# Scores of two layers as eight small TensorE tiles: four batches over four PSUM banks a step

## What is computed

```python
def layer(x, ctx, mask, Wq, Wk, Wv, Wo, gamma, beta, gate):   # x, ctx: (64, 64, 256)
    a = layer_norm(ctx, gamma, beta)
    Q, K, V = (heads(t @ W.T) for t, W in ((x, Wq), (a, Wk), (a, Wv)))   # 16 heads of 16 features
    scores = einsum('bhtd,bhsd->bhts', Q, K) * 16 ** -0.5
    attn = softmax(where(mask, scores, -inf), axis=-1)
    out = einsum('bhts,bhsd->bhtd', attn, V)
    return x + tanh(gate) * (out.reshape(x.shape) @ Wo.T)
```

## Time and profile before

| | |
|---|---|
| median of 3 runs | 643.26 us (642.9 to 643.43) |
| profiled execution: first to last instruction | 641.2 us |
| its own time | not listed apart; the runs are about 2.1 us above its span |
| PE busy | 612.8 us |
| DVE busy | 481.5 us |
| ACT busy | 486.4 us |
| one turn of the loop | 74.8 us |

### The profile page before, as it was taken

The page is one execution under the profiler, slowest core; times in us unless marked ns, Lnnn a source line. Parts: engine busy times, 40 slices in busy tenths (PEclk is TensorE's granted clock), DMA queues, the critical chain, the costliest instruction groups (busy, mean ns, idle before and its releaser), DMA issues.

```text
span 641.2 us, 22171 instructions
## 1 busy us (share of the span) xinstructions
PE 612.8 (96%) x9027; PEld 556.5 (87%) x9027; DVE 481.5 (75%) x1069; ACT 486.4 (76%) x945; POOL 119.4 (19%) x136
## 2 busy tenths in 40 slices
PE   1799999999999999999999999999999999999996
PEld 1688899989898898988999898988989899899885
DVE  4866778785986869777787859868697777876475
ACT  0998778776876969767787768869697677877682
POOL 3602420007010060104300070100601043000000
PEclk9999999999999999999999999999999999999999
DMA  5420002000021000110020000200001100000001
GB/s 159 143 71 2 3 3 73 9 28 2 2 73 34 2 1 24 51 34 2 2 73 13 23 2 2 73 34 2 2 17 56 35 2 1 3 14 23 3 2 34
DMA packets 18485, 18.09 MB, mean 28 GB/s; under 512 B 1828, under 2 KB 18340, under 8 KB 18404
## 3 DMA queue, kind: packets, MB, share of 16 engines
q1 hardware_dynamic: 18024, 16.55, 8.1%
q0 software_dynamic: 320, 0.26, 0.3%
q10 hardware_dynamic: 60, 0.01, 0.0%
HBM read 12.63 MB, written 4.19 MB: 26 GB/s over the span
## 4 chain that ended last, share of the span: by engine, by line
PE 88%; ACT 7%; DMA 2%; issue 1%; DVE 1%; SPq 1%; DVEq 0%; ACTq 0%
PE psum L394 13%; PE psum L396 11%; PE psum L395 11%; PE psum L626 10%; PE psum L702 10%; PE psum L646 8%; PE psum L695 4%; PE psum L614 4%; PE psum L636 3%; PE psum L535 2%; PE psum L523 2%; PE psum L498 2%; PE psum L460 2%; PE psum L506 2%; PE psum L531 1%
## 5 line engine op out<-in xcount | busy, mean ns | idle before, releaser
L1027 DVE TENSOR_TENSOR shifted<-psum,negmax 128x512 f32<-128x512 f32 x128 | 88.5, 691 | 9.8 <-ACT work L825 4.9
L825 ACT ACTIVATE work<-shifted 128x512 f32<-128x512 f32 x128 | 78.1, 642 | 19.9 <-DVE shifted L1027 19.6
L1023 DVE TENSOR_REDUCE negmax<-psum 128x8 f32<-128x512 f32 x128 | 87.3, 682 | 4.7 <-PE psum L626 4.5
L842 ACT ACTIVATE work<-psum,group_mask 128x512 f32<-128x512 f32 x128 | 79.5, 698 | 2.1 <-PE psum L646 1.7
L626 PE MATMUL psum<-kbd,work 64*128 64x128 f32 x1024 | 69.7, 280 | 0.6 <-issue 0.4
L646 PE MATMUL psum<-const,work 64*128 64x64 f32 x1536 | 65.3, 225 | 4.2 <-issue 1.3
L702 PEld LDWEIGHTS psum<-v,work 128*64 128x64 f32 x2048 | 62.4, 138 | 6.8 <-issue 5.4
L646 PEld LDWEIGHTS psum<-const,work 64*128 64x128 f32 x1536 | 57.5, 140 | 10.5 <-issue 7.9
L626 PEld LDWEIGHTS psum<-kbd,work 64*128 64x128 f32 x1024 | 61.9, 188 | 5.2 <-issue 3.3
L702 PE MATMUL psum<-v,work 128*64 128x34 f32 x2048 | 66.1, 225 | 0.0
L786 ACT ACTIVATE work<-psum,const 128x512 f32<-128x512 f32 x64 | 40.6, 685 | 20.8 <-PE psum L396 20.6
(11 more groups left out here) (185 smaller groups left out, 1661.3 us busy)
## 6 DMA issues: line engine op xcount, KB each, us to landing
x_raw<-in_x_dram SPq DMA_DIRECT2D x8, 512.0 KB, 4.2
c_raw<-in_ctx_dram SPq DMA_DIRECT2D x8, 512.0 KB, 4.9
out_dram<-attn SPq DMA_DIRECT2D x16, 256.0 KB, 2.1
mrow_u<-in_mask_dram SPq DMA_DIRECT2D x8, 64.0 KB, 5.0
kbd<-in_L_xattn_Wq_dram SPq DMA_DIRECT2D x2, 256.0 KB, 6.7
kbd<-in_L_xattn_Wk_dram SPq DMA_DIRECT2D x2, 256.0 KB, 7.2
kbd<-in_L_xattn_Wv_dram SPq DMA_DIRECT2D x2, 256.0 KB, 7.4
kbd<-in_L_xattn_Wo_dram SPq DMA_DIRECT2D x2, 256.0 KB, 8.0
```

The source lines that it names most:

```text
L825: act.activation(e, shifted[:, i % 2, :].rearrange("t (c k) -> t c k", c=NK), ACT.Exp).then_inc(exps, 1)
L842: act.activation(probsT[:, at, :], o[:], ACT.Copy, scale=group_mask[:, i:i + 1]).then_inc(free, 1)
L1023: dve.tensor_reduce(negmax[:, i % 2, :], sv, AX_X, ALU.max, negate=True).then_inc(rowmax, 1)
L1027: dve.tensor_tensor(shifted[:, i % 2, :].rearrange("t (j k) -> t j k", k=C), sv, negmax[:, i % 2, :].unsqueeze(2).broadcast_to([P, NJ, C]) ...
```

## The change

In layers one and two PE's tiles become 32 rows x 64 columns: two heads of one batch. The queries are copied once and unmasked (`queries`), the keys carry the mask by head parity and the scale (`parity` instead of `own_row`), so that their two versions are the two heads of a strip. One step fills four banks, one for each strip of 32 rows, with four batches (two pairs) in each; S(l, i) to S(l, i+3) are computed together. A bank has the two batches of a pair on the upper and lower 64 partitions. The transposes read four rows of `probs` (of which there are eight now) for a pair; the keys of two heads lie on the 128 partitions, `v2` is block-diagonal in the head instead of the batch, and the mask is set by batch instead of by pair. The weighting's counts and shapes stay. The copy of V out of PSUM becomes four instructions of 64 partitions x 256 instead of two of 64 x 512. Heads come out in natural order, and the sorted copy of Wo in the prologue goes.

```diff
-    o += X(1, 1) + X(1, 2) + S(1, 4) + S(1, 5) + copied("V1", 1) + X(1, 3) + T(1, 0) + S(1, 6) + S(1, 7) + X(1, 4) + T(1, 1)
+    o += X(1, 1) + X(1, 2) + copied("V1", 1) + X(1, 3) + T(1, 0) + S(1, 4) + S(1, 5) + S(1, 6) + S(1, 7) + X(1, 4) + T(1, 1)
...
-    o += p("K2", 1) + p("Q2", 0) + p("O1", 1) + H(3) + p("V2", 0) + L(3) + S(2, 0) + S(2, 1) + X(2, 0) + S(2, 2) + S(2, 3)
-    o += p("Q2", 1) + X(2, 1) + copied("Q2", 1) + X(2, 2) + p("K3", 1) + f("V0", 1) + X(2, 3) + T(2, 0) + S(2, 4) + S(2, 5)
-    o += T(2, 1) + f("xT", 0) + f("xT", 1) + X(2, 4) + S(2, 6) + S(2, 7) + X(2, 5) + p("V2", 1) + f("Mn", 0) + f("Mn", 1)
+    o += p("K2", 1) + p("Q2", 0) + p("O1", 1) + H(3) + p("V2", 0) + L(3) + S(2, 0) + S(2, 1) + S(2, 2) + S(2, 3) + X(2, 0)
+    o += p("Q2", 1) + X(2, 1) + copied("Q2", 1) + X(2, 2) + p("K3", 1) + f("V0", 1) + X(2, 3) + T(2, 0) + S(2, 4) + S(2, 5) + S(2, 6) + S(2, 7)
+    o += T(2, 1) + f("xT", 0) + f("xT", 1) + X(2, 4) + X(2, 5) + p("V2", 1) + f("Mn", 0) + f("Mn", 1)
...
+    def rows_of(order):
+
+        return {s[1:]: n % 8 for n, s in enumerate(s for s in order if s[0] == "X" and s[1] < 3)}
...
-                    for c in range(NK):
-                        for h in range(2):
-                            for to, done, rows in ((o, signal, slice(0, C)), (o2, signal2, slice(C, 2 * C))):
-                                dst = to[:, D * c:D * c + D].rearrange("t (r h s) -> t r h s", r=2, h=2)[:, :, h, :]
-                                mm_ = pe.matmul(dst, qe[rows, c, i + h].rearrange("p q t -> p (q t)"),
-                                                kbd[l - 1][rows, c, i + h], start=True, stop=True)
-                                if c == NK - 1 and h == 1:
-                                    mm_.then_inc(done, 1)
+                    strips = [(o, signal)] + [start_fill(g, ("S", l, i + r), last) for r in range(1, 4)]
+                    for n in range(2 * NK):
+                        p, k = n // NK, n % NK
+                        for r, (to, done) in enumerate(strips):
+                            rows = slice(32 * r, 32 * r + 32)
+                            for c in range(2):
+                                b = i + 2 * p + c
+                                mm_ = pe.matmul(to[C * c:C * c + C, P * n:P * n + P], queries[rows, k, C * b:C * b + C],
+                                                kbd[l - 1][rows, k, b].rearrange("p q s -> p (q s)"), start=True, stop=True)
+                            if n == 2 * NK - 1:
+                                mm_.then_inc(done, 1)
                     return
...
-                    pe.wait_ge(exps, 18 * g + (8 * (l - 1) + 2 * i + 2))
-                    at = 2 * slot(g, l, i, last)
-                    e = probs[:, at:at + 2, :].rearrange("t a (j k) -> t (a j) k", k=P)
-                    turn_halves((o, o2), (signal, signal2), [e[:, j, :] for j in range(NJ)])
+                    pe.wait_ge(exps, 18 * g + (8 * (l - 1) + 4 * (i // 2) + 4))
+                    turn_halves((o, o2), (signal, signal2),
+                                [probs[:, exp_row(g, l, 4 * (i // 2) + r, last), D * (i % 2) + P * k:D * (i % 2) + P * k + P]
+                                 for k in range(NK) for r in range(4)])
...
-                    for h in range(2):
-                        rows = slice(C * h, C * h + C)
-                        ins = act.activation(v2[int(name[1]) - 1][rows, 2 * i:2 * i + 2, :, h, 0:HD],
-                                             o[rows, :].rearrange("k (q n v) -> k q n v", q=2, n=NH), ACT.Copy)
+                    values = v2[int(name[1]) - 1][:, 4 * i:4 * i + 4].rearrange("k (p c) j q v -> k c q p j v", c=2)
+                    for c in range(2):
+                        for q in range(2):
+                            ins = act.activation(values[C * q:C * q + C, c, q, :, :, 0:HD],
+                                                 o[C * c:C * c + C, :].rearrange("k (p j q v) -> k q p j v", p=2, q=2, v=HD)[:, q], ACT.Copy)
...
-                    for q in range(2):
-                        ins = act.activation(qe[:, :, 4 * i:4 * i + 4, q, :], o[:].rearrange("p (k b t) -> p k b t", k=NK, t=C),
-                                             ACT.Identity, scale=parity[:, q:q + 1])
-                    ins.then_inc(free, 1)
+                    act.activation(queries[:, :, HALF * i:HALF * i + HALF], o[:].rearrange("p (k t) -> p k t", k=NK),
+                                   ACT.Copy).then_inc(free, 1)
...
-                        act.activation(probsT[:, at, :], o[:], ACT.Copy, scale=group_mask[:, i:i + 1]).then_inc(free, 1)
+                        act.activation(probsT[:, at, :], o[:], ACT.Copy, scale=group_mask[:, 2 * i + c:2 * i + c + 1]).then_inc(free, 1)
...
-                for m in range(NK):
-                    ins = pool.tensor_copy(o_sorted[l - 1][:, m, :].rearrange("o (q j d) -> o q j d", q=2, d=HD),
-                                           raw[f"o{l}"][:, m, :].rearrange("o (j q d) -> o q j d", q=2, d=HD))
-                ins.then_inc(o_sorted_ready, 1)
```

More of the change, by code:

```diff
@@ L165, in slot, with exp_row @@
         return (SLOT_PRO if g is None else SLOT_LAST if last else SLOT)[l, u]
+    def rows_of(order):
+        return {s[1:]: n % 8 for n, s in enumerate(s for s in order if s[0] == "X" and s[1] < 3)}
+    ROW, ROW_LAST, ROW_PRO = rows_of(ORDER), rows_of(LAST_ORDER), rows_of(PROLOGUE)
+    def exp_row(g, l, i, last):
+        return (ROW_PRO if g is None else ROW_LAST if last else ROW)[l, i]
     def ahead(g, per):
@@ L263, in build @@
         beta_row = scratch[:, 11:13]
-        v2 = [sb(f"v2_{l}", [P, NP, NH, 2, VW]) for l in (1, 2)]
-        qe = work[:, 8:12, :].rearrange("p a b -> p (a b)").rearrange("p (k b q t) -> p k b q t", k=NK, b=GB, q=2)
+        v2 = [sb(f"v2_{l}", [P, GB, NJ, 2, VW]) for l in (1, 2)]
+        queries = work[:, 12:14, :]
         negmax = sb("negmax", [P, 2, NJ])
@@ L269, in build @@
         wo3T = shifted[:, :, 0:D]
-        probs = work[:, 0:4, :]
-        probsT = work[:, 4:8, :]
+        probs = work[:, 0:8, :]
+        probsT = work[:, 8:12, :]
         recip = sb("recip", [P, 2, NH])
         recip0 = sb("recip0", [P, 2, 4])
-        attn = sb("attn", [P, NP, 2, NJ, HD])
+        attn = sb("attn", [P, NP, NH, HD])
         attnT = pair_of("attnT", [P, 2, HALF])
@@ L594, in scores_step @@
                 _, l, i = step
-                if l < 3 and i % 2:
+                if l == 0 and i % 2 or l in (1, 2) and i % 4:
                     return
@@ L599, in scores_step @@
                     used = fronts("Mn", "Mm")
-                elif l < 3 and l and i % 4 == 0:
+                elif l < 3 and l:
                     used = [("P", f"Q{l}", i // 4)]
@@ L700, in weighted_step @@
                 for j in range(NJ):
-                    for q in range(2):
-                        mm_ = pe.matmul(o[C * q:C * q + C, 2 * VW * j:2 * VW * (j + 1)], probsT[:, at + q, C * j:C * j + C],
-                                        v2[l - 1][:, i, 2 * j + q].rearrange("k b v -> k (b v)"), start=True, stop=True)
+                    for c in range(2):
+                        mm_ = pe.matmul(o[C * c:C * c + C, 2 * VW * j:2 * VW * (j + 1)], probsT[:, at + c, C * j:C * j + C],
+                                        v2[l - 1][:, 2 * i + c, j].rearrange("k q v -> k (q v)"), start=True, stop=True)
                 mm_.then_inc(signal, 1)
@@ L807, in set_mask @@
             def set_mask(g):
+                act.wait_ge(mask_turned, 1)
                 act.sem_inc(act_held, 1)
-                act.activation(group_mask[:], mask_col[:, bass.ds(NP * g, NP)], ACT.Copy).then_inc(mask_set, 1)
+                act.activation(group_mask[:].rearrange("k (p c) -> k p c", c=2), mask_keys[:, bass.ds(NP * g, NP), :], ACT.Copy).then_inc(mask_set, 1)
             def exp_step(g, step, last):
@@ L817, in exp_step @@
                     for u in range(2):
-                        ins = act.activation(probs[:, 2 * slot(g, 0, i // 2, last) + i % 2, D * u:D * u + D], psum[bk][:, D * u:D * u + D], ACT.Exp,
+                        ins = act.activation(probs[:, exp_row(g, 0, i, last), D * u:D * u + D], psum[bk][:, D * u:D * u + D], ACT.Exp,
                                              bias=negmax0[:, i, u:u + 1])
@@ L822, in exp_step @@
                     act.wait_ge(freed[bk], released(bk, n))
-                    at = 2 * slot(g, l, i // 2, last)
-                    e = probs[:, at:at + 2, D * (i % 2):D * (i % 2) + D]
-                    act.activation(e, shifted[:, i % 2, :].rearrange("t (c k) -> t c k", c=NK), ACT.Exp).then_inc(exps, 1)
+                    act.activation(probs[:, exp_row(g, l, i, last), :], shifted[:, i % 2, :], ACT.Exp).then_inc(exps, 1)
                 else:
@@ L1105, in weight_step @@
                     dve.tensor_tensor(ident_half[:], ident[:, 0:C], ident[:, C:P], ALU.add).then_inc(ident_ready, 1)
```

(6 more changed lines are left out.)

65 lines of the change are left out of this document (30 added, 35 removed).

## The result

The changed kernel takes 711.65 us in the median of four runs (705.23 to 712.85), the kernel before 643.16 in the same session (642.9 to 643.43). The ratio is 1.1045, with a 95% interval of 1.102 to 1.1069: slower, by 68 us. The prediction's sum was 694.2, with a range of 678 to 722.

The account below looks back on a forecast made before the run. PE alone was taken to set the time before, a PE-DVE-ACT chain after: 8 groups x (3.86 + 2.57) = 51.4, less 0.5, +50.9 on a 641.2 span, 692.1; plus 2.1 gives 694.2 us, range 678 to 722.

Parts of the forecast that it names:

- The score products: Layers' score bursts: eight tiles run at once, 64 records in 8 rounds, 1.17 us a burst.
- (b): Rival, score bursts: longer, up to 2.06 us, on the chain four times a group; 723, or half, 709; chance 0.18.
- PE's saving: Score bursts: about 0.9 us each, four a group, 3.6 us, 29 in all; not subtracted, turns into waiting.
- The new wait: Transposes need four banks' exps, second burst queues behind T(1,0): +3.86 us a group in layer one, +2.57 in layer two.
- DVE's wait for the second burst: Layer one: DVE idles after the fourth shift until the second burst's banks are ready, 3.4 us a group.
- (c): Rival: PE at lower clock after the 4.0 us wait; 12 us, 706; in both layers 24, 718; chance 0.09.
- The prologue: Before the loop: Wo's sorting on GpSimd goes, four small DVE mask copies come; -0.5 us, ends -1.0 and +0.3.
- (a): Main case: the chain as summed, spread from V's copy and hand-overs, 686 to 706 us; chance 0.62.
- (e): Rival: the waits for exps don't arise and PE's 29 us saving stands, 614 us; chance 0.04.
- (d): Rival, layer two: ACT earlier than counted, half of 2.57 x 8 less, 684, or none of it, 674; chance 0.07.

Follow-up runs that it names:

- constant products: Changed kernel plus 14 constant products ahead of T(1,0)'s wait for the exps and 7 ahead of T(2,0)'s, results overwritten: 702.01 us.
- the pair with equal order: Order of the reordered small tiles, two layer-two exps moved behind transposes, run with 64x128 and with 32x64 tiles: 679.74 and 659.46 us.
- The order with the old tiles: Kernel before with its own 64x128 tiles, but the changed kernel's step order and gate of four exps: 714.01 us.
- the reordered small tiles: Changed kernel with another step list: V3(1) and second score burst ahead of T(1,0), V1(1) copied behind first exp, layer two reordered: 654.38 us.
- the small tiles of the pair: The reordered small tiles with layer two's fifth and seventh exps moved behind the transposes: 659.46 us, ratio 1.0233.
- the fastest kernel of all: Kernel before, its tiles and gate of two exps unchanged, with V3(1), V0(1), V2(1) and K3(1) moved in the list: 638.77 us.
- the late copy and constant products: Changed kernel with V1(1) copied behind the fourth exp, and 11 constant products ahead of T(1,0), 7 ahead of T(2,0): 701.91 us.
- The kernel with large tiles: Tiles, bank views and copies of the kernel before, in the same order and gate as the small tiles of the pair: 679.74 us.

## Why the prediction was right, and where it was off

It said slower, by a chain in which one engine works at a time, and named its links. Taken from the start of the burst, for layer one:

| link | predicted | measured |
|---|---|---|
| burst of four banks | 1.17 | 1.21 |
| fourth shift ends | +6.56 | +6.53 |
| V1(1) copied in four pieces | 1.57 | 1.56 |
| T(1,0) starts | +8.15 | +8.25 |
| PE waits there | 4.0 | 4.04 |
| T(1,2) starts, at full clock | +16.12 | +16.25 (constant products) |
| PE waits at T(1,2), at full clock | 1.8 | 1.80 (constant products) |
| layer one longer, at full clock | 3.86 | 3.8 (constant products) |
| layer one longer, mean of eight | 3.86 | 5.48 |
| PE waits at T(2,0) | 2.4 | 2.38 |
| layer two and the way back longer | 2.57 | 2.83 |

**The score products.** Right: eight tiles run together, 64 records in 1.21 us. The rival of a burst of 1.6 to 2.06 (b) falls. PE's saving is real too, by the pair with equal order: 3.3 us of busy time a turn at full clock, where 3.6 were counted, and 2.9 us of the turn.

**The new wait.** Right in both layers. The order with the old tiles shows that the gate and the order make it. Two totals agree better than their parts, by luck. The waits of the transposes on exps are 65.9 us, where 66 were predicted; but T(1,2) waited 1.47 us in the mean instead of 1.8, and the last group's layer two 2.6 us more than its 2.4. PE's busy share is 85%, 84% predicted; but 607.7 us were busy instead of 584, in a span 19 us longer. DVE's wait for the second burst, 3.4 predicted, is 3.93 to 4.79 in layer one of the changed kernel and 3.41 with constant products, where PE kept its clock.

**The clock.** This is the term that was mis-sized. The sum held it at nothing; as a rival (c) it had 0.09 and 12 us for layer one. The runs give 31.70 - 30.0 = 1.7 us a group there, 14 us. The mean granted clock of 0.956 over 711 us is about 63 us at 1.2 GHz. The prediction set the prologue's row aside because the view printed 1.00 there. That reading was wrong: in the trace of the kernel before, the records of the granted clock begin only at 24.8 us, and the view counts the time ahead of them as 1.00. In the changed kernel 16 such records take 0.71 or 1.12 by the clock, so the row's 1.12 pointed to the lower level.

**The last group.** The sum priced it like the others. From layer two on it lost 3.7 us instead of 2.57. It has no front work of a next group between its gates, and the clock fell there too; how much each made was not taken apart.

**The prologue.** Predicted -0.5, measured +2.6. Where the clock stays up, the first burst starts at 57.9 in the reordered small tiles and at 58.6 in the small tiles of the pair, 0.35 us before and 0.4 behind the old time; the predicted -0.5 is no more than that spread. In the profiled run of the changed kernel it came at 60.9 because a clock of 0.5 was granted from 24.5 on, after two waits of PE:

```profile
18.12 3.38 PE L597 MATMUL psum<-const,kbd 128*128 128x128 f32 x16 [1.44 <-DMA kbd<-in_L_xattn_Wo_dram]
...
23.48 0.46 PE L566 MATMUL psum<-w0T,attn 128*128 128x128 f32 x2 [1.98 <-DVE attn L1200]
...
26.96 1.99 PE L508 MATMUL psum<-x_norm,w0T 64*64 64x256 f32 x16 [0.68 <-ACT x_norm L902]
```

L508 takes 1.09 in the loop for the same 16 records, and 1.13 at this place in the reordered kernel. From its start to the first burst it takes 33.9 us here and 31.9 in the kernel before, in the reordered small tiles and in the pair's. So 2.0 of the 2.6 us are the clock again and no work that the change added; the other 0.6 had come before.

Of the 18.9 us between the +50.9 predicted for the span and the +69.8 measured, 13.0 are layer one (13.6 of clock, less 0.6 at full clock), 3.1 the prologue, 1.8 layer two and the way back, and 1.1 the last group.

The rivals: 711.65 lies above (a)'s 706 as well. What happened is (a) and (c) together, which the list held as alternatives; (c) priced layer one's clock at 12 us, close to the 14 measured. (e), the saving stands, is out by 98 us; (d), layer two milder, is out (+2.83, not less than 2.57). What the prediction left unsaid, though its numbers held it, is that the loss hangs on the order of the list and not on the tiles: another order gave 57 of the 68 us back.

## What to carry to other kernels

A kernel whose PE is 96% busy can still have stretches in which two other engines are close to being the limit (here the eighth exp of layer one ends at 295.64, half a microsecond after PE began the transposes whose second half needs it); before making PE's part cheaper, write down when the operands of its next wait are ready, and if the new tiling makes a wait need more of them, put PE's independent work in front of that wait in the same edit. To learn what a tiling is worth, compare it with the old one in the same order of steps, and in more than one order: here it was 2.4 us in one and 20 in another, and the fastest kernel of all has the large tiles. And where buffers go round in a ring in the order of a list, moving one step changes the buffers of all behind it.

## What the runs showed of the hardware that was not expected

Short waits are enough to bring TensorE's clock down, and not always. Granted 0.50 followed a wait of 4.04 to 4.12 us in each group of the changed kernel, one of 2.94 with the large tiles in seven of eight groups, one of 1.79 to 1.80 in three groups of the changed kernel and one of 1.79 to 2.01 in each group with the late copy and constant products. After the same 1.80 in the kernel with constant products alone it stayed at 1.00 in five groups and fell in two. Two waits of 0.95 and 0.99 us, at T(1,0) and at the weighting behind it, come in each of the first seven groups of the reordered small tiles, and nearly so in the pair's small tiles; the clock fell behind them in one of the first seven groups of the former and three of the latter, and stayed at 1.00 in the others. In the timeline above T(1,0) still took 1.22 at 142.81, and the weighting at 145.02 took 1.93 for 32 records that take 1.13 elsewhere. The kernel with large tiles waited only the 0.99 at the same place, and stayed at 1.00 in these seven groups. Which of these histories ends in a lower clock stays open.

The Trainium skill ("TensorE: Matmul & The Clock Gate", Part 1) has the clock fall after idling and return with work. The traces agree. They add that in a full pipeline a few microseconds of waiting a turn are enough: layer one lost 14 us of 711 by it.

Eight tiles of 32 rows by 64 columns, loads included, went through in 1.21 us for 64 records: eight rounds took about what eight rounds of two large tiles had taken, 1.16. The Trainium skill ("TensorE: Matmul & The Clock Gate", Part 3) has a load overlap a matmul only in another row strip. Two tiles shared each strip here, and the trace shows no added time for their loads.
